# Attention: values moved by SyncE's transfers, heads n and n+8 in a pair, x and bias summed by GpSimd, x1 and logits from one operation of VectorE

## What is computed

```python
def attention(q, k, v, Wq, Wk, Wv, Wp, bp):       # 16 heads of 8
    qp, kp, vp = q @ Wq.T, rope(k @ Wk.T), rope(v @ Wv.T)
    weights = softmax(qh @ kh.T / sqrt(8))        # per sequence and head
    return concat(weights @ vh) @ Wp.T + bp
x = x + tanh(g_xattn) * attention(layernorm(x), ctx, ctx, ...)
z = layernorm(x)
w = softmax(top2(z @ gate_kernel))                # 8 experts, 2 chosen
x = x + tanh(g_ffn) * sum_e w[e] * ((silu(z @ w0[e]) * (z @ w1[e])) @ wo[e])
```

## Time and profile before

| | us |
|---|---|
| median of 3 runs | 549.7 |
| the profiled execution's own time | 547.75 |
| its span, first to last instruction | 545.9 |
| TensorE busy (matmul) | 517.3 |
| ScalarE busy | 428.2 |
| VectorE busy | 395.9 |
| GpSimd busy | 379.7 |

### The profile page before, as it was taken

One profiled execution on the slowest core, in us unless ns is written; L12 is line 12 of the kernel. 1 busy time (PEld: TensorE's weight loads), 2 busy tenths in 40 slices (PEclk: granted clock), 3 DMA queues, 4 the chain that ended last, 5 costly groups with the idle time before them and its releaser, 6 DMA issues.

```text
span 545.9 us, 21014 instructions
## 1 busy us (share of the span) xinstructions
PE 517.3 (95%) x6123; PEld 452.8 (83%) x6124; DVE 395.9 (73%) x1418; ACT 428.2 (78%) x1090; POOL 379.7 (70%) x524
## 2 busy tenths in 40 slices
PE   8999999999999999999999989999899999999960
PEld 6788788888888888888887778998899999999950
DVE  5789899999999999999999965474333333334774
ACT  3889899999999999999999967655556667777640
POOL 4246888777777877877777657777777777667670
PEclk9999999999999999999999999999999999999995
DMA  3821121121112112121211221334333343338997
GB/s 92 251 81 28 52 65 52 49 65 51 58 53 63 49 49 63 49 63 52 62 55 57 63 69 40 104 99 133 119 101 98 103 113 99 93 110 248 332 271 231
DMA packets 64242, 52.98 MB, mean 97 GB/s; under 512 B 8607, under 2 KB 60064, under 8 KB 64176
## 3 DMA queue, kind: packets, MB, share of 16 engines
q1 hardware_dynamic: 46560, 30.79, 20.1%
q0 software_dynamic: 8448, 16.93, 9.3%
q10 hardware_dynamic: 9168, 4.46, 2.8%
HBM read 29.44 MB, written 23.22 MB: 96 GB/s over the span
## 4 chain that ended last, share of the span: by engine, by line
PE 82%; issue 5%; DMA 4%; POOL 3%; DVE 2%; ACT 1%; SPq 1%; POOLq 0%; ACTq 0%; DVEq 0%
PE psH L602 18%; PE psK L582 12%; PE psH L482 7%; PE psG L497 5%; PE psH L497 5%; PE psH L488 5%; PE psK L618 5%; PE psO L618 5%; PE psK L470 5%; PE psX L463 3%; PE psO L516 2%; PE psO L517 2%; PE psO L475 2%; POOL results L1250 2%; PE psO L540 1%
## 5 line engine op out<-in xcount | busy, mean ns | idle before, releaser
L1250 POOL DMA_INDIRECT results<-ys,zin x136 | 134.4, 988 | 50.7 <-issue 42.2
L1177 POOL DMA_INDIRECT lists<-zp,dest x128 | 128.0, 1000 | 34.5 <-issue 26.5
L602 PE MATMUL psH<-zT,wcur 128*128 128x128 f32 (+1 forms) x760 | 131.1, 321 | 1.7 <-issue 0.7
L602 PEld LDWEIGHTS psH<-zT,wcur 128*128 128x128 f32 x760 | 109.4, 191 | 9.9 <-issue 2.0
L1082 DVE TENSOR_TENSOR hm<-psH,hs 128x512 f32<-128x512 f32 x68 | 47.0, 691 | 90.5 <-PE psH L602 48.2
L976 DVE TENSOR_REDUCE mx<-psH 128x8 fp32r<-128x512 f32 x128 | 82.4, 685 | 11.9 <-PE psH L482 10.5
L582 PEld LDWEIGHTS psK<-v,pT 128*64 128x64 f32 x2048 | 65.1, 138 | 25.8 <-issue 25.8
L695 ACT ACTIVATE ex<-psH,rs 128x512 f32<-128x512 f32 x128 | 84.4, 689 | 0.9 <-PE psH L488 0.5
L582 PE MATMUL psK<-v,pT 128*64 128x64 f32 x2048 | 73.8, 225 | 1.0 <-DVE ropA L1040 1.0
L756 ACT COPY wcur<-w 128x512 f32 x95 | 56.0, 616 | 23.4 <-issue 19.0
L746 ACT COPY v<-kvr 64x64 f32<-64x64 f32 x256 | 63.7, 249 | 2.2
(11 more groups left out here) (176 smaller groups left out, 1061.9 us busy)
## 6 DMA issues: line engine op xcount, KB each, us to landing
yy<-results SPq DMA_DIRECT2D x16, 512.0 KB, 4.9
zin<-lists SPq DMA_DIRECT2D x41, 130.0 KB
out_dram<-x ACTq DMA_DIRECT2D x16, 256.0 KB
xring<-in_x_dram SPq DMA_DIRECT2D x31, 128.0 KB
cring<-in_ctx_dram SPq DMA_DIRECT2D x31, 128.0 KB
zin<-lists SPq DMA_DIRECT2D x54, 65.0 KB
results<-ys,zin POOLq DMA_INDIRECT x136
w<-in_L_ffn_w_kernel_dram SPq DMA_DIRECT2D x2, 1024.0 KB, 7.0
```

What stands on the lines that cost most here:

```text
L602: last = pe.matmul(bank[t.buf(2)][:, k * ET + c.start:k * ET + c.stop], wcur[:, t.buf(2), h, a, k * P:(k + 1) * P], zT[:, t.buf(2), c], st ...
L1177: nc.gpsimd.indirect_dma_start(lists, bass.IndirectOffsetOnAxis(ap=dest[:, t.buf(4), j:j + 1], axis=0), zp[:, t.buf(4), j, :], None).then_ ...
L1250: nc.gpsimd.indirect_dma_start(results, bass.IndirectOffsetOnAxis(ap=zin[:, t.buf(8), h, D:D + 1].bitcast(U32), axis=0), ys[:, t.buf(8), h ...
```

## The change

Pairs are heads n and n+8, so that a tile's values need no interleaving: v9 keeps, per sequence and buffer, 64 columns of values of the first eight heads, 64 of the last eight, and 64 of ones and zeros, 192 in all. The value product reads three runs of 8 columns (24 and not 64), and the softmax's exponentials and the scaled output are written in the order that this asks for. SyncE moves the values with four DMAs per tile, 64 partitions x 256 bytes each (`values`), for which v9_in takes the place of v9_done. GpSimd adds bias to x for two tiles at a time into the new tile xb (`biased`), so the product with the identity goes, and the gate's 8 columns stay; a load now waits for xb_done as well, since biased reads xring. VectorE adds xb to 136 columns of psO in one operation, and ScalarE copies the 8 logits from x1.

```diff
-VW = 2 * (DH + 1)
-VPAD = 64
-VROW = (PAIRS - 1) * VW + VPAD
+VW = 3 * DH
+VROW = PAIRS * VW
...
-        x1 = sb("x1", [P, NT, D])
+        x1 = sb("x1", [P, NT, XW])
         logit = sb("logit", [P, 4, XW - D])
         cring = sb("cring", [P, 4, D])
         xring = sb("xring", [P, 4, D])
+        xb = sb("xb", [P, 8, XW])
         ident = sb("ident", [P, P])
...
+                    wait_for(sp, xb_done, t + 1, back=4)
 
                 def load(t):
 
                     carry(sp)
                     sp.dma_start(xring[:, t.buf(4):t.buf(4) + 2, :], two(x_d, t)).then_inc(tiles_in, 16)
                     sp.dma_start(cring[:, t.buf(4):t.buf(4) + 2, :], two(c_d, t)).then_inc(tiles_in, 16)
+
+                def values(t):
+                    wait_for(sp, kvr_done, t)
+                    carry(sp)
+                    wait_for(sp, pv_ps, t, back=4)
+                    carry(sp)
+                    for b in range(2):
+                        for c in range(2):
+                            sp.dma_start(v9[c * S:(c + 1) * S, t.buf(4), b, c * D // 2:(c + 1) * D // 2],
+                                         kvr[b * S:(b + 1) * S, t.buf(2), D + c * D // 2:D + (c + 1) * D // 2]).then_inc(v9_in[t.buf(2)], 16)
 
...
-                for t in range(2, 8, 2):
+                for t in range(2, 6, 2):
                     load_ready(Tile(4, None, t))
                     load(Tile(4, None, t))
+                sp.wait_ge(ones_ready, 1)
+                values(Tile(4, None, 0))
+                values(Tile(4, None, 1))
+                load_ready(Tile(4, None, 6))
+                load(Tile(4, None, 6))
                 sp.dma_start(w01[:, :, 0, :], A["L0_ffn_w0_kernel"].rearrange("e d h -> d e h")).then_inc(experts_in, 16)
                 sp.dma_start(w01[:, :, 1, :], A["L0_ffn_w1_kernel"].rearrange("e d h -> d e h")).then_inc(experts_in, 16)
+                values(Tile(4, None, 2))
                 for e in range(E):
                     sp.dma_start(wo[:, e, :, :], A["L0_ffn_wo_kernel"][e].rearrange("(k h) d -> h k d", k=2)).then_inc(experts_in, 16)
                 sp.wait_ge(e_const, 8)
                 for n in range(SPARE):
                     sp.dma_start(lists[E * CAP + n * ET:E * CAP + (n + 1) * ET, :].rearrange("(p h) c -> p h c", h=2), pad[:, :, :]).then_inc(spare_out, 16)
+                values(Tile(4, None, 3))
                 with sp.Fori(2, NT // 4) as turn:
                     for u in (0, 2):
-                        wait_for(sp, kvr_done, Tile(4, turn, u - 3))
-                        carry(sp)
+                        values(Tile(4, turn, u - 4))
+                        values(Tile(4, turn, u - 3))
                         load_ready(Tile(4, turn, u))
                         load(Tile(4, turn, u))
...
+                for t in (NT - 4, NT - 3):
+                    values(Tile(4, None, t))
...
+                    if t == NT - 6:
+                        for n in (NT - 2, NT - 1):
+                            values(Tile(4, None, n))
...
-                            for g in (2 * h, 2 * h + 1):
+                            for g in (h, h + 2):
                                 r, c = slice(32 * g, 32 * g + 32), slice(b * S, (b + 1) * S)
-                                last = pe.matmul(psH[h][c, g % 2, 0:256], qT[r, t.buf(2), c], kmask[r, t.buf(2), :, c],
+                                last = pe.matmul(psH[h][c, g // 2, 0:256], qT[r, t.buf(2), c], kmask[r, t.buf(2), :, c],
...
-                        pe.matmul(psO[:, 368:368 + XW], xcT[:, t.buf(8), 0:P], idg[:, :], start=True, stop=False, skip_group_check=True)
-                        pe.matmul(psO[:, 368:368 + XW], oT[:, t.buf(2), :], wTg[:, :], start=False, stop=True, skip_group_check=True).then_inc(attn_ps, 1)
+                        pe.matmul(psO[:, 368:368 + XW], oT[:, t.buf(2), :], wTg[:, :], start=True, stop=False, skip_group_check=True)
+                        pe.matmul(psO[:, 368 + D:368 + XW], xcT[:, t.buf(8), 0:P], gatec[:, :], start=False, stop=True, skip_group_check=True).then_inc(attn_ps, 1)
...
-                        wait_for(pe, v9_done, t)
+                        wait_slot(pe, v9_in, t, 64)
...
-                                last = pe.matmul(psK[b * S:(b + 1) * S, 2 * D + n * VW:2 * D + n * VW + VPAD], pT[:, t.buf(2), n // 4, o:o + S],
-                                                 v9[:, t.buf(4), b, n * VW:n * VW + VPAD], start=True, stop=True)
+                                last = pe.matmul(psK[b * S:(b + 1) * S, 2 * D + n * VW:2 * D + (n + 1) * VW], pT[:, t.buf(2), n // 4, o:o + S],
+                                                 v9[:, t.buf(4), b, :].rearrange("p (j n w) -> p j n w", j=3, w=DH)[:, :, n, :],
+                                                 start=True, stop=True)
                         last.then_inc(pv_ps, 1)
...
+                def logits(t):
+                    wait_for(act, x1_done, t)
+                    wait_for(act, lg_sb, t, back=4)
+                    nc.scalar.copy(logit[:, t.buf(4), :], one(x1, t)[:, D:XW]).then_inc(logit_done, 1)
...
                     def exponentials(t, h):
-                        nc.scalar.activation(ex[:, t.buf(2), h, :].rearrange("p (g c) -> p g c", g=2), psH[h][:, :, 0:256],
+                        nc.scalar.activation(ex[:, t.buf(2), h, :].rearrange("p (n c k) -> p c n k", c=2, k=S),
+                                             psH[h][:, :, 0:256].rearrange("p c (n k) -> p c n k", k=S),
                                              ACT.Exp, scale=rs[:, t.buf(4) // 2, t.buf(2):t.buf(2) + 1]).then_inc(exp_done[h], 1)
...
+                    if t := ATT_ACT.at(s, -4):
+                        logits(t)
...
-                    if t := ATT_ACT.at(s, -1):
-                        wait_for(act, kvr_done, t)
-                        wait_for(act, pv_ps, t, back=4)
-                        for b in range(2):
-                            for c in range(2):
-                                src = kvr[b * S:(b + 1) * S, t.buf(2), D:2 * D] \
-                                    .rearrange("p (n c w) -> p n c w", c=2, w=DH)[:, :, c, :]
-                                dst = v9[c * S:(c + 1) * S, t.buf(4), b, 0:PAIRS * VW] \
-                                    .rearrange("p (n c w) -> p n c w", c=2, w=DH + 1)[:, :, c, 0:DH]
-                                last = nc.scalar.copy(dst, src)
-                        last.then_inc(v9_done, 1)
...
-                        o = psK[:, 2 * D:2 * D + PAIRS * VW].rearrange("p (h w) -> p h w", w=DH + 1)
-                        nc.vector.reciprocal(rden[:, :], o[:, :, DH]).then_inc(rden_done, 1)
+                        o = psK[:, 2 * D:2 * D + VROW].rearrange("p (n j w) -> p j n w", n=PAIRS, w=DH)
+                        nc.vector.reciprocal(rden[:, :].rearrange("p (c n) -> p n c", c=2), o[:, 2, :, 0:2]).then_inc(rden_done, 1)
                         wait_for(dve, rden_done, t)
-                        nc.vector.tensor_tensor(on[:, t.buf(2), :].rearrange("p (h w) -> p h w", w=DH), o[:, :, 0:DH],
-                                                rden[:, :].unsqueeze(2).broadcast_to([P, H, DH]), ALU.mult).then_inc(on_done, 1)
+                        nc.vector.tensor_tensor(on[:, t.buf(2), :].rearrange("p (c n w) -> p c n w", c=2, w=DH), o[:, 0:2, :, :],
+                                                rden[:, :].rearrange("p (c n) -> p c n", c=2).unsqueeze(3).broadcast_to([P, 2, PAIRS, DH]),
+                                                ALU.mult).then_inc(on_done, 1)
...
-                        nc.vector.tensor_tensor(logit[:, t.buf(4), :], psO[:, 368 + D:368 + XW], bpg[:, D:XW], ALU.add).then_inc(logit_done, 1)
-                        nc.vector.tensor_tensor(one(x1, t), psO[:, 368:368 + D], bpg[:, 0:D], ALU.add).then_inc(x1_done, 1)
+                        wait_for(dve, xb_done, t + (1 - t.buf(2)))
+                        nc.vector.tensor_tensor(one(x1, t), psO[:, 368:368 + XW], xb[:, t.buf(8), :], ALU.add).then_inc(x1_done, 1)
...
+                def biased(t):
+                    if t.turn is None and t.k == 1:
+                        pool.wait_ge(first_in, 32)
+                        pool.wait_ge(bias_ready, 1)
+                    rows_in(pool, t)
+                    wait_for(pool, x1_done, t, back=8)
+                    carry(pool)
+                    nc.gpsimd.tensor_tensor(xb[:, t.buf(8) - 1:t.buf(8) + 1, 0:D], xring[:, t.buf(4) - 1:t.buf(4) + 1, :],
+                                            bpg[:, 0:D].unsqueeze(1).broadcast_to([P, 2, D]), ALU.add).then_inc(xb_done, 2)
...
-                        wait_for(pool, v9_done, t, back=2)
+                        wait_slot(pool, v9_in, t, 64, back=2)
                         nc.gpsimd.tensor_tensor(kvr[:, t.buf(2), :], ropA[:, t.buf(2), :], ropB[:, t.buf(2), :],
                                                 ALU.add).then_inc(kvr_done, 1)
+                    if (t := ATT_POOL.at(s, 4)) and t.buf(2):
+                        biased(t)
```

(4 more changed lines are left out.)

24 lines of the change are left out of this document (11 added, 13 removed).

## The result

The changed kernel takes 563.56 us (median of 4 runs, 562.52 to 565.58) against 549.48 for the kernel before on the same chip: ratio 1.0252, 95% interval 1.0230 to 1.0274. The forecast was 554.3, the range 548.5 to 560.5. The direction was right and the size was not: +14.1 us where +4.6 stood.

The account below looks back on a forecast made before the run. It took TensorE's own instructions to bound the steady attention stage, single small steps the start. TensorE -2.6, GpSimd +0.7 and start +6.5 sum to +4.6 us: 554.3 us from the median of 549.7, range 548.5 to 560.5.

Parts of the forecast that it names:

- TensorE, -2.6 us: Attention stage: narrower value product ends 31 ns sooner per tile, identity's removal saves at most 10 ns, over 63 tiles.
- matmul width paces the value product: Rival, value product on TensorE: 24 moving columns instead of 64 save time, 532 us; milder form 548.9; 6% each.
- ScalarE and VectorE, 0: Attention stage: copies leaving ScalarE and VectorE's changed additions gain nothing, since TensorE's full row covers them.
- GpSimd, +0.7 (0 to 1.5): Additions of 0.72 us every second tile cost +0.7 us where GpSimd also scales wo and issues scatters.
- what is added to GpSimd costs nothing while its 24% of slack covers it: Steady part of attention: GpSimd's additions, 0.36 us per tile, fit within its idle time and cost 0.
- The start, +6.5 (2 to 12): First tiles of attention: SyncE's value transfers, in one line with all loads, delay the value products by 6.5 us.
- I take 0.45: SyncE's queue: issuing one piece (one of four value transfers per tile) takes 0.45 us, near the small loads' pace.
- Step 1: Start, tile 0's pieces landed at 16.8: kvr of tile 2 runs from 16.85 to 17.6, wanted at 18.84, hidden.
- Step 2: Start: w goes at 21.1, tile 2's pieces land behind it at 30.3, wanted at 26.34, so 4.0 us late.
- Step 3: Start: wo and pad rows hold SyncE, tile 3's pieces land at 37.6 against 31.12: +6.5 us in all.
- Step 4: Start: tile 4's pieces hidden; load of tiles 8 and 9 out at 41.1, transpose at 43.6, just hidden: 0.
- SyncE is slower than thought: Rival, SyncE's queue: pieces at wo's pace, start +12, load of tiles 8 and 9 no longer hidden: 560 to 563, 12%.

Follow-up runs that it names:

- piece2_first: The changed kernel with tile 2's four value transfers issued ahead of the expert weights w, tile 3's still behind wo and the pad rows: 565.12 us, ratio 1.0255.

## Why the prediction was wrong, step by step

- **TensorE, -2.6 us.** Right in mechanism and a little small: 37 ns a tile for the width (31 put down), 22 for the identity (at most 10), so -3.7. The rival "matmul width paces the value product" is out: 32 loads still span 1.01 us. The page "TensorE: Matmul & The Clock Gate" of the Trainium skill makes a load's time follow the number of weight columns (LDWEIGHTS), and the trace agrees: with 64 weight columns the span is the same for 64 and for 24 moving columns.
- **ScalarE and VectorE, 0.** Right: 4.779 us a tile with the copies and without.
- **GpSimd, +0.7 (0 to 1.5).** Right at the place named (+0.6 at tile 11, +1.1 by tile 14), too small in the whole: 3.0 us net, 4.4 with the identity's gain added back. That includes the late steps, whose share in a typical run is open. The step "what is added to GpSimd costs nothing while its 24% of slack covers it" also overrated the slack.
- **The start, +6.5 (2 to 12): the step that failed**, by its sizes and in part by its path. It measured 11.9 us, at tile 4.
  - "I take 0.45" for a piece: the pieces of tiles 0 to 2 took 0.78 and 0.95 us on average, with one of 1.86 and one of 1.81 among ten of 0.53 to 0.68. I chose the small loads' pace over wo's 0.875, and in the start the truth lay at wo's.
  - Step 1 asked whether kvr of tile 2 was in time and did not carry on to tile 0's own product, which wanted its pieces at 16.85; they were put at 16.8, with nothing to spare, and TensorE got them 1.8 us late.
  - Step 2 had tile 2 at 4.0 late; it was 8.6: the second half of w was issued at 24.2 and not 22.4, took 8.9 us to land and not 7.8, and tile 2's last piece was there 1.8 us behind it and not 0.1.
  - The clock: after a stop of 7 us TensorE runs at half clock until 42.4, and the step of tile 3 takes 8.2 us, 3.4 too many; no term had it.
  - Step 3 had tile 3 wait for pieces that land at 37.6. They landed at 39.8, but nothing waited for them: the path ran through tile 2 and the clock. At the full clock the two paths would have met there (34.95 + 4.75 = 39.7, an estimate from the trace), and piece2_first shows step 3's wait once tile 2 is relieved.
  - Step 4 held: no stop at tiles 4 to 8, though its load was out at 46.6 and not 41.1. The aside that tile 2's pieces would land at 27.0 if they overtook w should read 26.4 by its own terms; they did not overtake it.
- **The rival that came nearest** is "SyncE is slower than thought" (12%, 560 to 563): pieces at wo's pace and a start of +12, as measured. That the total lay near its end is partly luck: 3.4 us of the 12 are the clock's, its second condition (step 4 no longer fits) did not come true, and the late steps, which it does not have, made up for that.
- **Not in the text at all:** the late steps, where a code load meets a scatter and the clock may be halved behind the stop: in the profiled pair 5.3 us at tiles 53, 61 and 63, and an expert stage 1.8 us longer where the same length was expected. The kind stood in the earlier trace rows, as the landing of 4.03 us at 62.90, which I read as GpSimd being behind; 1.5 us of it were the last share.

## What to carry to other kernels

When work goes to a queue, count the whole line in front of every deadline, at the pace of that queue's slowest like kind, and begin with the deadline of the first tile. To put one transfer first only hands the wait to the next; what helps is fewer issues (one transfer for eight) and loads moved out of the tight stretch. An engine off the critical path has less slack than its idle share says if others wait for its results in program order. And if the busiest engine of a stage is full, freeing the second one buys nothing.

## What the hardware showed that was not expected

- Where a 16 KB load of program code had just ended, one share of a scatter came up to 2.1 us behind the others; no trace has such a share where the engines were in their loop and loaded no code.
- Waits that are already met, as instructions of their own, follow each other on TensorE every 108 ns (64 and 128 in a row), and the first product came 82 to 98 ns later for each.
- In the changed kernel an SBUF to SBUF transfer of 16 KB takes SyncE 0.46 to 1.85 us to issue, 0.59 in the median; a load of 64 or 128 KB from HBM takes 0.38 (x) and 0.42 (ctx) in the median.
- After a stop of 6.98 us TensorE came back at half clock; the same 32 passes took 1.91 us and not 1.12. At the end of the stage stops of 1.1 to 1.9 us had a stretch at half clock with them in 13 traces of 13.
- wo's eight issues took 4.4, 5.4, 7.0 and 8.7 us in four traces, the same instructions each time.
